# Front end of a fused attention and feed-forward kernel in another order: bv, AqT, Gram of batch 1, and x of batch 0 in two DMAs

## The chip, the core and the metric

The kernel runs on one NeuronCore of one Trainium2 chip; the seven others are idle. The metric is the device time of one execution in microseconds (us), lower is better. Times in the profile are in us from the start of the span, which is the time from the first to the last instruction.

## What is computed

The input x is [8, 1024, 128] (batch, sequence, channels), all in float32. A layer of linear attention and a feed-forward layer follow each other, each with a residual and a layer norm. Cut to what matters:

```python
q, k1, k2, v1, v2 = [heads(x + x @ W.T + b) for W, b in (...)]   # 16 heads of 8 channels
S1 = einsum('bhnd,bhne->bhde', k1, v1) / n                       # 8 x 8 for each head
S2 = einsum('bhnd,bhne->bhde', k2, v2) / n
S12 = S1 * S2
out = q @ S1 * mean(v2) * g1 + S12.sum(2) * g2 + q @ S2 * mean(v1) * g3 + q @ S12 * g4
a = layernorm(out) * ln_g + ln_b
x = layernorm(x + a @ Wo.T + bo)
tgt2 = relu(x @ w1[0] + b1[0]) @ w2[0] + b2[0]                   # the routing always picks expert 0
x = layernorm(x + layernorm(x + tgt2) * gamma + beta)
```

Neither k nor v is ever computed for a row of x. With A = I + W.T, S1 is made of A.T G A and the bias, where G = x.T x is the 128 x 128 Gram matrix of a batch, with the column sums of x beside it. So each batch has a small preparation (G, then E = G A plus a bias part, V the sums of v, S, a matrix M, and the folded matrix "PQ" for q and the output), and then a product of x with PQ for every row.

## The kernel before

**Tiling.** Each batch is 8 tiles of 128 rows; a step handles a group of 4 tiles (512 rows), 16 steps in all, from n = 0 to 15. They are preceded by two steps of preparation, n = -2 and n = -1, which are the front end. Every engine has its own instruction stream written by hand; what orders the streams among each other is semaphores alone. A float32 matmul or transpose on TensorE appears in the profile as two instructions, except the `transpose` calls, which are one instruction each.

**TensorE in step -2** (`body`, lines 1182 to 1203): ten warm-up matmuls on the identity (`keep_warm(10)`), as soon as `ident` is made; the Gram products of batch 0 for tiles 0 to 3 (`gram(0, ...)`, which waits for x of batch 0); the transposes of the four k and v weights (`turn_kv`); the Gram products of tiles 4 to 7; `gram_av(0)`, which multiplies G with A_kv; `turn_vectors` (waits for all small vectors: spreads the bv rows over 128 partitions by a product with ones, transposes the biases and spreads the g factors); `turn_x(0)`, four transposes of x for the first product; `turn_o` (Wo); `turn_late` (ln_g, ln_b, b1); `keep_warm(2)`; `ak_e(0)`, which gives the raw S; `output_rows`, two products from the turned Wo (u and zw); `gram(1)`, the Gram products of batch 1, in bank `up_ps[2]`; `attention_matrix(0)`, M with AqT; `gram_av(1)`; `centered(0)`, the product with the centering matrix, which gives PQ; `ak_e(1)`. In step -1 three tiles of `gram(2)` come before `product(0, 0)`, the first product of x with PQ, and then `turn_x(1)`, the rest of `gram(2)`, `gram(3)`, `attention_matrix(1)`, half of `gram(4)`, `centered(1)` and `turn_x1(0)`, which turns the normalized x1 for the feed-forward part.

**VectorE in step -2**: A_kv from the turned weights (lines 769 to 771); then it waits for `vec_turned` and copies g_rows and the first three columns of `cols`; `e_and_v(0)` (E, line 854, needs `bv_rows`, V, line 861, needs `nbv_rows`); `factors` (a column of AqT, line 779, the other columns of `cols`, and the sum AqT = Wq + I, line 783); `prepare(dve, 0)` (gv, then S of batch 0 in `s_out`, then S12, T, S12g and M); `u_row`, `xT_rest(0)`, `e_and_v(1)`, `PQ_rest(0)` (the two lower parts of PQ, lines 818 and 819), `s_out(1)`.

**ScalarE in step -2**: G of batch 0 to SBUF (`gram_out(0)`), the three copies of bv (`less_bv`), the upper part of x transposed (`xT_upper(0)`), `output_weights` (lnb_wide, WoT, Wog, and at its end the wait for zw and `center`), `gram_out(1)`, then the copy of PT (`PT_copy`) and of the upper part of PQ (`PQ_upper`).

**GpSimd**: constants, eight DMAs (Wo, Wq, bo, b2, beta, gamma, w1, w2), then the head mask times g (`gmask`, needs `cols_ready`), then x + u for the first two groups (`xu`), and the preparation of batch 1.

**DMA queues**: SyncE issues x of batch 0, Wk1, Wk2, ln_g, ln_b, b1 and x of batches 1 to 7, in this order. ScalarE issues Wv1, Wv2, bk1, bk2, bq, bv1, bv2 and four g vectors. The issuing instructions run in order on the engine's sequencer.

## Time and profile before

| what | value |
|---|---|
| median of 3 runs | 204.87 us (204.83 to 205.17) |
| profiled execution, its own time | 204.72 us |
| its span | 203.0 us |
| busy: TensorE matmul / VectorE / ScalarE / GpSimd | 94% / 78% / 64% / 70% |
| TensorE's share of the chain that ended last | 85% |
| memory traffic | 6.17 MB read, 4.20 MB written |

"Busy" is the share of the span in which an engine executes; waits are not in it. TensorE's matmul and its weight loads overlap each other, and matmuls are pipelined, so that the distance from one start to the next is shorter than one's duration. A row of the timeline merges like instructions that follow each other; the time in brackets is the idle time of the engine before the row, with the instruction that ended it. "SPq" and "ACTq" are the sequencers that issue DMAs.

### The profile page before, as it was taken

The numbers are of one execution on the slowest core, as the hardware profiler recorded it, in microseconds if no ns is written. First come the engines' busy times: TensorE is split into PE (matmuls) and PEld (weight loads), VectorE is DVE, ScalarE is ACT, GpSimd is POOL, SyncE is SP. The second block draws the span as 40 slices with busy tenths as digits, with TensorE's granted clock in tenths as the row PEclk, the third lists the DMA queues.
The fourth block names the chain that finished last, engine by engine and source line by source line (L and its number), as shares of the span: only waits on it lengthen the run. The fifth ranks groups of instructions, "written<-read, shape, count | busy, mean of one in ns | idle before, by whom it ended". The sixth has DMA issues, their size and how long they took to land.

```text
span 203.0 us, 4316 instructions
## 1 busy us (share of the span) xinstructions
PE 191.2 (94%) x1381; PEld 174.8 (86%) x1381; DVE 157.6 (78%) x471; ACT 129.2 (64%) x386; POOL 141.2 (70%) x190
## 2 busy tenths in 40 slices
PE   6899999999999999999999999999999999999920
PEld 6788997989898999999997989898989899987820
DVE  0186745987869887898879896989698969897683
ACT  0342538372859665975758675967597759786852
POOL 8526662676489838986599759985998598877350
PEclk9999999999999999999999999999999999999985
DMA  5999501200001000101001300100010101011012
GB/s 151 238 243 288 143 0 27 58 0 5 0 0 55 37 15 5 53 0 52 3 16 51 117 2 0 53 28 28 0 55 2 52 3 52 2 52 40 15 53 103
DMA packets 12624, 10.64 MB, mean 52 GB/s; under 512 B 713, under 2 KB 10458, under 8 KB 12602
## 3 DMA queue, kind: packets, MB, share of 16 engines
q1 hardware_dynamic: 11944, 9.32, 15.2%
q0 software_dynamic: 352, 0.92, 2.5%
q8 instruction: 11, 0.18, 0.4%
q10 hardware_dynamic: 306, 0.13, 0.2%
q14 instruction: 11, 0.09, 0.2%
HBM read 6.17 MB, written 4.20 MB: 51 GB/s over the span
## 4 chain that ended last, share of the span: by engine, by line
PE 85%; DVE 6%; issue 3%; ACT 2%; POOL 2%; DVEq 0%; POOLq 0%; ACTq 0%
PE up_ps L1024 26%; PE down_ps L1024 25%; PE z_ps L1024 14%; PE prep_ps L1024 12%; PE turn_ps L1177 4%; PE turn_ps L1148 3%; DVE st L793 1%; DVE down_ps L844 1%; POOL y2g L548 1%; POOL y L552 1%; DVE z_ps L904 1%; ACT res L667 1%; DVE y2n L800 1%; DVE res L1001 0%; DVE y L986 0%
## 5 line engine op out<-in xcount | busy, mean ns | idle before, releaser
L1024 PE MATMUL down_ps<-w_sb,hT 128*128 128x128 f32 x480 | 58.9, 276 | 0.1
L1024 PEld LDWEIGHTS down_ps<-w_sb,hT 128*128 128x128 f32 x480 | 56.4, 192 | 0.7 <-ACT hT L685 0.3
L685 ACT ACTIVATE hT<-up_ps,cols 128x512 f32<-128x512 f32 x64 | 42.2, 682 | 5.2 <-PE up_ps L1024 5.0
L667 ACT ACTIVATE res<-y,nb,rstd 128x128 f32<-128x128 f32 x60 | 24.8, 483 | 6.6 <-POOL nb L516 5.9
L574 POOL TENSOR_TENSOR x1b<-x,b_rows 128x512 f32<-128x512 f32 x16 | 20.5, 1284 | 10.6 <-DVE x L800 10.6
L1024 PE MATMUL up_ps<-x1T_hi,w_hi 128*128 128x512 f32 x64 | 26.1, 408 | 0.0
L1024 PE MATMUL up_ps<-x1T_lo,w_hi 128*128 128x512 f32 x64 | 25.4, 398 | 0.0
L1024 PE MATMUL up_ps<-x1T_hi,w_lo 128*128 128x512 f32 x64 | 25.3, 395 | 0.0
L548 POOL TENSOR_TENSOR y2g<-y2n,gamma_rows 128x512 f32<-128x512 f32 x15 | 19.2, 1281 | 4.9 <-DVE y2n L800 4.9
L800 DVE TENSOR_SCALAR x<-z_ps,st,rstd 128x128 f32<-128x128 f32 x64 | 21.9, 405 | 0.1
L634 ACT ACTIVATE z_sq<-z_ps 128x128 f32<-128x128 f32 x64 | 16.8, 270 | 7.6 <-PE z_ps L1024 7.6
L800 DVE TENSOR_SCALAR y2n<-down_ps,st,rstd 128x128 f32<-128x128 f32 x60 | 21.0, 405 | 0.5
L563 POOL TENSOR_TENSOR xu<-X,u_rows 128x512 f32<-128x512 f32 x16 | 18.9, 1186 | 3.2 <-DVE u_rows L789 3.2
L576 POOL TENSOR_TENSOR x1beta<-x,beta_rows 128x512 f32<-128x512 f32 x16 | 20.6, 1291 | 0.0
L552 POOL TENSOR_TENSOR y<-y2g,x1beta 128x512 f32<-128x512 f32 x15 | 19.1, 1272 | 1.2
L1024 PE MATMUL z_ps<-PQ_hi,xT_hi 128*128 128x256 f32 x64 | 19.3, 302 | 0.0
L904 DVE SCALAR_TENSOR_TENSOR z_ps<-z_ps,rstd,xu 128x128 f32<-128x128 f32 x64 | 18.2, 353 | 0.6
L1024 PE MATMUL z_ps<-PQ_hi,xT_lo 128*128 128x256 f32 x64 | 18.0, 282 | 0.0
L1024 PE MATMUL z_ps<-PQ_lo,xT_hi 128*128 128x256 f32 x64 | 17.9, 280 | 0.0
L1024 PE MATMUL z_ps<-PQ_hi,spread 128*128 128x256 f32 x64 | 17.9, 280 | 0.0
L626 ACT ACTIVATE std<-st,eps_col 128x4 f32<-128x4 f32 x46 | 12.4, 295 | 7.3 <-DVE st L793 7.3
L733 ACT ACTIVATE x1T_hi<-turn_ps 128x512 fp32r<-128x512 f32 x16 | 9.4, 589 | 11.1 <-PE turn_ps L1148 10.9
(170 smaller groups left out, 418.3 us busy)
## 6 DMA issues: line engine op xcount, KB each, us to landing
X<-in_L_attn_x SPq DMA_DIRECT2D x8, 512.0 KB, 8.7
out<-res SPq DMA_DIRECT2D x15, 256.0 KB, 2.0
V_all<-V_dram SPq DMA_DIRECT2D x6, 128.0 KB, 3.1
w_sb<-in_L_ffn_w POOLq DMA_DIRECT2D x2, 256.0 KB, 8.4
out<-res SPq DMA_DIRECT2D x2, 128.0 KB, 2.2
w_raw<-in_L_attn_Wv ACTq DMA_DIRECT2D x2, 64.0 KB, 2.7
w_raw<-in_L_attn_Wk SPq DMA_DIRECT2D x2, 64.0 KB, 3.9
w_raw<-in_L_attn_Wo POOLq DMA_DIRECT2D x1, 64.0 KB, 3.0
```

Source lines behind the costliest of these rows:

```text
L548: pool.tensor_tensor(y2g[:, :, :], y2n[:, :, :], rows(gamma_rows[:, :]), ALU.mult).then_inc(y2g_out, 1)
L552: pool.tensor_tensor(y3[(s - 1) % 2][:, :, :], y2g[:, :, :], x1beta[(s - 1) % 2][:, :, :], ALU.add).then_inc(y3_out, 1)
L563: pool.tensor_tensor(xu[s % 2][:, :, :], X[:, b, g * TILES:(g + 1) * TILES, 0:C], rows(u_rows[:, :]), ALU.add).then_inc(xu_out, 1)
L574: pool.tensor_tensor(x1b2[(s + 1) % 2][:, :, :], x1[:, :, :], rows(b2_rows[:, :]), ALU.add).then_inc(x1b2_out, 1)
L576: pool.tensor_tensor(x1beta[(s + 1) % 2][:, :, :], x1[:, :, :], rows(beta_rows[:, :]), ALU.add).then_inc(x1beta_out, 1)
L626: act.activation(dst[:, :], src, ACT.Sqrt, bias=eps_col[:, :], scale=scale).then_inc(done, 1)
L634: act.activation(z_sq[:, t, :], z_ps[t // 2][:, t % 2 * 256:t % 2 * 256 + C], ACT.Square, accum_out=z_sum[:, t:t + 1]).then_inc(sq_out, 1)
L667: last = act.activation(res[buf][:, t, :], y3[buf][:, t, :], ACT.Identity, scale=rstd4[:, t:t + 1], bias=nb4[:, t:t + 1])
L685: act.activation(hT[:, k, :], up_ps[k % len(up_ps)][:, :], ACT.Relu, bias=cols[:, 5 + k:6 + k]).then_inc(relu_out, 1)
L800: last = dve.tensor_scalar(dst[:, t, :], of_tile(t), st[:, t // 2, 3 * (t % 2) + 1:3 * (t % 2) + 2], rstd[:, t:t + 1], ALU.subtract, ALU.mult)
L904: last = dve.scalar_tensor_tensor(out=y1_tile(t), in0=y1_tile(t), scalar=rstd1[:, t:t + 1], in1=xu[(s + 1) % 2][:, t, :], op0=ALU.mult, op ...
L1024: return pe.matmul(o, lhsT, rhs, start=start, stop=stop)
```

## The change

- x of batch 0 is loaded by two DMAs of four tiles each. The second has its own semaphore, `x0_second`, which the second Gram half and GpSimd's second `xu` wait for.
- On ScalarE's queue the two bv rows are issued ahead of bk1, bk2 and bq, with their own semaphore; the product that spreads them (`spread_bv`) moves from `turn_vectors` to the place between the second Gram half and the wait for A_kv.
- TensorE: six warm-up matmuls instead of ten, `keep_warm(2)` gone, `turn_vectors` behind `turn_x(0)` and `turn_o`, `gram(1)` ahead of `output_rows`, `gram_av(1)` ahead of `attention_matrix(0)`, two tiles of `gram(2)` ahead of `centered(0)` and two behind `ak_e(1)` instead of three there.
- VectorE: g_rows and the first three columns of `cols` are copied after E and V of batch 0, S and S12 of batch 0 come before gv, and the column of AqT is copied between them.
- GpSimd computes the sum AqT = Wq + I, after its DMA issues and before `gmask`.
- ScalarE: `gram_out(1)` comes before the copy of zw to `center`.

```diff
+            def values():
+                eng.wait_ge(masks_ready, 1)
+                eng.tensor_tensor(gv[:, :, :], v_of(b), gmask[:, 0:2, :], ALU.mult).then_inc(m_step, 1)
+
+            def scores():
+                eng.wait_ge(S_out, b + 1)
+                eng.tensor_tensor(S12[:, :], S_sb[:, 0, :], S_sb[:, 1, :], ALU.mult).then_inc(m_step, 1)
+
             if b == 0:
                 s_out(eng, 0)
-            eng.wait_ge(S_out, b + 1)
-            eng.tensor_tensor(S12[:, :], S_sb[:, 0, :], S_sb[:, 1, :], ALU.mult).then_inc(m_step, 1)
+                scores()
+                eng.tensor_copy(AqT[:, C:C + 1], cols[:, 2:3]).then_inc(AqT_ready, 1)
+                values()
+            else:
+                values()
+                scores()
...
-            load_x(0)
+            half = SEQ_TILES // 2
+            sp.dma_start(X[:, 0, 0:half, 0:C], x_v[0, :, 0:half, :]).then_inc(x_loaded[0], 16)
+            sp.dma_start(X[:, 0, half:SEQ_TILES, 0:C], x_v[0, :, half:SEQ_TILES, :]).then_inc(x0_second, 16)
...
+            pool.wait_ge(consts, 2)
+            pool.wait_ge(qo_loaded, 16 * 2)
+            pool.tensor_tensor(AqT[:, 0:C], w_raw[:, 5, :], ident[:, :], ALU.add).then_inc(AqT_ready, 1)
             pool.wait_ge(const_set, 4)
...
+            for i, v in enumerate((bv1, bv2)):
+                act.dma_start(bv_row[:, i, :], row(v)).then_inc(bv_loaded, 16)
             for i, v in enumerate((bk1, bk2, bq)):
                 act.dma_start(vec_rows[i:i + 1, :], row(v)).then_inc(vec_loaded, 16)
-            for i, v in enumerate((bv1, bv2)):
-                act.dma_start(bv_row[:, i, :], row(v)).then_inc(vec_loaded, 16)
...
+            def center_weights():
+
                 act.wait_ge(zw_done, 1)
                 act.activation(center[:, 1, :], zw_ps, ACT.Copy).then_inc(zw_ready, 1)
...
                     gram_out(1)
+                    center_weights()
...
-            dve.wait_ge(vec_turned, 1)
-            dve.tensor_copy(g_rows[:, :, :].rearrange("p i h -> p (i h)"), vec_ps[:, 3:67])
-            dve.tensor_copy(cols[:, 0:3], vec_ps[:, 0:3]).then_inc(cols_ready, 1)
 
             def factors():
 
-                dve.wait_ge(cols_ready, 1)
-                dve.tensor_copy(AqT[:, C:C + 1], cols[:, 2:3])
+                dve.wait_ge(vec_turned, 1)
+                dve.tensor_copy(g_rows[:, :, :].rearrange("p i h -> p (i h)"), vec_ps[:, 3:67])
+                dve.tensor_copy(cols[:, 0:3], vec_ps[:, 0:3]).then_inc(cols_ready, 1)
                 dve.wait_ge(late_turned, 1)
                 dve.tensor_copy(cols[:, 3:9], late_ps).then_inc(late_ready, 1)
-                dve.wait_ge(qo_loaded, 16 * 2)
-                dve.tensor_tensor(AqT[:, 0:C], w_raw[:, 5, :], ident[:, :], ALU.add).then_inc(AqT_ready, 1)
+                dve.wait_ge(cols_ready, 1)
...
+            def spread_bv():
+
+                pe.wait_ge(bv_loaded, BV_VECTORS)
+                mm(bv_ps, ones[0:1, :], bv_row[:, :, :].rearrange("p j c -> p (j c)")).then_inc(bv_done, 1)
+
             def turn_vectors():
 
                 pe.wait_ge(vec_loaded, VECTORS)
-                mm(bv_ps, ones[0:1, :], bv_row[:, :, :].rearrange("p j c -> p (j c)")).then_inc(bv_done, 1)
...
-                    keep_warm(10)
+                    keep_warm(6)
                     pe.wait_ge(consts, 2)
                     gram(0, range(0, 4))
                     turn_kv()
                     gram(0, range(4, SEQ_TILES))
+                    spread_bv()
                     pe.wait_ge(A_ready, 1)
                     gram_av(0)
-                    turn_vectors()
                     turn_x(0)
                     turn_o()
+                    turn_vectors()
                     turn_late()
-                    keep_warm(2)
                     ak_e(0)
+                    gram(1, range(SEQ_TILES))
                     output_rows()
-                    gram(1, range(SEQ_TILES))
+                    gram_av(1)
                     attention_matrix(0)
-                    gram_av(1)
+                    pe.wait_ge(nbv_ready, 1)
+                    gram(2, range(0, 2))
                     centered(0)
                     ak_e(1)
                     return
                 if st.n == -1:
-                    pe.wait_ge(nbv_ready, 1)
-                    gram(2, range(0, 3))
+                    gram(2, range(2, 4))
                     product(0, 0)
                     turn_x(1)
-                    gram(2, range(3, SEQ_TILES))
+                    gram(2, range(4, SEQ_TILES))
```

## Rows read from the trace of the kernel before

**Rows 1.** Page: chain that ended last, shares by engine

```profile
PE 85%; DVE 6%; issue 3%; ACT 2%; POOL 2%; DVEq 0%; POOLq 0%; ACTq 0%
```

**Rows 2.** Timeline: start, us, engine, line, operation, tiles, count, [idle <-releaser]

```profile
0.94 0.64 SPq L430 DMA_DIRECT2D X<-in_L_attn_x  x1
...
1.58 4.28 PE L1024 MATMUL up_ps<-ident 128*128 128x128 f32 x20 [1.58 <-POOL ident L476]
...
1.63 1.11 SPq L436 DMA_DIRECT2D w_raw<-in_L_attn_Wk  x2
...
3.76 13.25 SPq L430 DMA_DIRECT2D X<-in_L_attn_x  x6
```

**Rows 3.** DMA issues: tile, queue, count, KB each, us from issue to landing

```profile
X<-in_L_attn_x SPq DMA_DIRECT2D x1, 512.0 KB, 4.9
...
w_raw<-in_L_attn_Wk SPq DMA_DIRECT2D x2, 64.0 KB, 3.9
...
X<-in_L_attn_x SPq DMA_DIRECT2D x1, 512.0 KB, 6.5
```

**Rows 4.** Timeline: Gram of batch 0, weight transposes, G out, gram_av(0)

```profile
5.95 1.13 PE L1024 MATMUL prep_ps<-X 128*128 128x130 f32 x8
...
6.92 0.60 PE L1034 MATMUL z_ps<-ident,w_raw 128*128 128x128 f32 x4
...
7.35 1.06 PE L1024 MATMUL prep_ps<-X 128*128 128x130 f32 x8
...
8.45 0.28 ACT L680 ACTIVATE G_sb<-prep_ps 128x130 f32<-128x130 f32 x1 [1.82 <-PE prep_ps L1024]
...
8.87 1.10 PE L1024 MATMUL prep_ps<-A_kv,G_sb 128*128 128x256 f32 x4 [0.46 <-ACT G_sb L680]
```

**Rows 5.** Timeline: bv products, E and V of batch 0

```profile
9.90 0.69 PE L1024 MATMUL up_ps<-bv_row,ones 1*128 1x256 f32 x2
...
11.13 0.48 DVE L854 SCALAR_TENSOR_TENSOR E_sb<-bv_rows,G_sb,prep_ps 128x256 f32<-128x256 f32 x1
...
11.53 0.42 DVE L861 TENSOR_TENSOR V_sb<-prep_ps,nbv_rows 128x256 f32<-128x256 f32 x1
```

**Rows 6.** Timeline: the last warm-up pair, AqT's column, ak_e(0)

```profile
11.66 0.71 PE L1024 MATMUL up_ps<-ident 128*128 128x128 f32 x4
...
11.86 0.14 DVE L779 COPY AqT<-cols 128x1 f32<-128x1 f32 x1
...
12.21 0.61 PE L1024 MATMUL prep_ps<-E_sb,A_kv 128*128 128x128 f32 x4
```

**Rows 7.** Timeline: mask on GpSimd; gv, S, T and M_sb on VectorE

```profile
11.37 1.07 POOL L505 TENSOR_TENSOR gmask<-g_rows,head_mask 128x512 f32<-128x512 f32 x1 [3.65 <-DVE cols L774]
...
12.55 0.43 DVE L372 TENSOR_TENSOR gv<-V_sb,gmask 128x256 f32<-128x256 f32 x1
...
12.93 0.61 DVE L359 SCALAR_TENSOR_TENSOR S_sb<-V_sb,cols,prep_ps 128x128 f32<-128x128 f32 x2
...
13.89 0.42 DVE L378 TENSOR_TENSOR T_sb<-S_sb,gv 128x256 f32<-128x256 f32 x1
...
15.01 0.29 DVE L383 TENSOR_TENSOR M_sb<-M_half,S12g 128x128 f32<-128x128 f32 x1
```

**Rows 8.** Timeline: attention matrix, PT, centered product, second PQ split

```profile
15.46 0.39 PE L1024 MATMUL prep_ps<-AqT,M_sb 128*128 128x130 f32 x2
...
16.00 0.28 ACT L654 ACTIVATE PT_sb<-prep_ps 128x130 f32<-128x130 f32 x1
...
16.95 1.03 PE L1024 MATMUL prep_ps<-center,PT_sb 128*128 128x256 f32 x4
...
19.10 0.43 DVE L819 TENSOR_TENSOR PQ_hi<-prep_ps,PQ_hi 64x256 fp32r<-64x256 f32 x1
```

**Rows 9.** Windows: stretch, us, busy by engine (instructions), PEclk, DMA share, GB/s

```profile
194.00:196.00 2.00, 0.19 (x2) 0.00 (x0) 1.60 (x5) 1.16 (x4) 0.98 (x3) 1.00 0.05 14
```

**Rows 10.** Timeline, TensorE's weight loads: transposes of x1 and their wait

```profile
26.91 0.42 PEld L1148 LDWEIGHTS turn_ps<-ident,x 128*128 128x128 f32 x4 [0.36 <-DVE x L800]
```

More of the change, by code:

```diff
@@ L175, in build @@
         kv_loaded = sem("kv_loaded")
+        bv_loaded = sem("bv_loaded")
         bv_done = sem("bv_done")
@@ L187, in build @@
         ffn_rows = sem("ffn_rows")
+        x0_second = sem("x0_second")
         x_loaded = [sem(f"x_loaded{b}") for b in range(BATCHES)]
@@ L369, in prepare @@
             wait(eng, pt_done, b)
-            eng.wait_ge(masks_ready, 1)
             k = b * 4
-            eng.tensor_tensor(gv[:, :, :], v_of(b), gmask[:, 0:2, :], ALU.mult).then_inc(m_step, 1)
+            def values():
[4 more added lines that the diff above has]
+                eng.tensor_tensor(S12[:, :], S_sb[:, 0, :], S_sb[:, 1, :], ALU.mult).then_inc(m_step, 1)
             if b == 0:
                 s_out(eng, 0)
-            eng.wait_ge(S_out, b + 1)
-            eng.tensor_tensor(S12[:, :], S_sb[:, 0, :], S_sb[:, 1, :], ALU.mult).then_inc(m_step, 1)
+                scores()
[4 more added lines that the diff above has]
+                scores()
             wait(eng, m_step, k + 2)
@@ L418, in run_steps @@
                 body(Step(n))
-        VECTORS = 16 * (4 + 3 + 2)
+        VECTORS = 16 * (4 + 3)
+        BV_VECTORS = 16 * 2
         LATE_VECTORS = 16 * 3
@@ L559, in body @@
                     pool.wait_ge(x_loaded[b], 16)
+                    if n == -1:
+                        pool.wait_ge(x0_second, 16)
                     if st.n == -2:
@@ L1063, in gram @@
                 pe.wait_ge(x_loaded[b], 16)
+                if b == 0 and tiles[0] >= SEQ_TILES // 2:
+                    pe.wait_ge(x0_second, 16)
                 if b == 3:
@@ L1120, in attention_matrix @@
                 wait(pe, M_out, (b + 1) * 2)
-                pe.wait_ge(AqT_ready, 1)
+                pe.wait_ge(AqT_ready, 2)
                 mm(prep_ps[:, 0:XW], M_sb[:, :], AqT[:, :], start=True, stop=False)
```

## The prediction

> **What bounds the kernel now.** I read the chain of work that ended last first: TensorE carries 85% of it [rows 1]. From about 28 us on TensorE has hardly a gap, so the steady state is a fixed amount of matmul work that starts when the front end lets it. The change touches the front end alone, and the amount of steady work is the same. So the question is by how much the first product on x (`product(0, 0)`) moves, and whether the shift survives until the dense part. Every time below is of the profiled execution, 204.72 us around its span of 203.0; the median of the runs shown is 204.87, 0.15 above it, and I subtract the shift from the median.
>
> Then I read the timeline of the front end by the row that each TensorE group waits for. In order: TensorE warms up on `ident` from 1.58 to 5.86, and x of batch 0 lands 4.9 after its issue at 0.94, at 5.84 [rows 2, 3]. The Gram products follow at 5.95, the four weight transposes at 6.92, the second half of the Gram at 7.35; G leaves ScalarE at 8.73 and lets `gram_av(0)` start at 8.87 [rows 4]. Behind it stand the bv products at 9.90; their copies hold back E until 11.13 and V until 11.53, 1.2 us after the products that E reads were over [rows 5]. Then comes a pair of warm-up matmuls, `ak_e(0)` at 12.21 [rows 6], VectorE's chain to M_sb at 15.30 [rows 7], and from M_sb the chain attention matrix, PT copy, centered product, PQ split, first product [rows 8]. Nearly all of it is one dependent chain of small steps, with TensorE, VectorE and ScalarE taking turns.
>
> **The change, part by part.**
>
> *x in two DMAs, ten warm-ups to six.* The first half must land before the transposes can be late because of it. The whole transfer takes 4.9 from issue, a transfer of 64 KB behind it 3.9 [rows 3]; so a half of 256 KB takes between 3.9 and 4.9, and lands at 4.8 to 5.8. The issue pitch of such a DMA is 0.69 (0.94 to 1.63) [rows 2], so Wk, the small rows and x of batches 1 to 7 are issued up to 0.69 later. Six warm-ups are twelve instructions at 4.28 / 20 = 0.214 each: TensorE is through at 4.2 and idle for 0.6 to 1.6. What binds next is `turn_kv`, which needs both Wk. Of the pair issued in 1.63 to 2.74 the second starts near 2.3 and lands 3.9 later, at 6.2 [rows 2, 3]. It stands behind x in the same queue, so either the queue's bytes set its landing (6.2 again) or its issue does (6.9). I take 6.2, since 64 KB taking 3.9 looks like waiting behind the 512 KB. The first Gram half is then hidden: from 4.8, eight instructions at 0.21 end at 6.5, at 0.11 at 5.7; with the clock rising in between as before, just under 6.2. The transposes start at 6.2 + 0.1 = 6.3 instead of 6.92, with the startup of the first one some 0.1 lost; the second Gram half comes at 6.82 instead of 7.35, and G and with it `gram_av(0)` at 8.35 instead of 8.87: **−0.52**. If Wk lands at 6.9, this step gives +0.1 to +0.2 instead. A_kv moves with the transposes and stays ahead of G, which is what the matmul row names as releaser [rows 4].
>
> The clock: the twenty warm-up instructions run at a pitch of 0.21, the later ones of the same kind at (7.35 − 6.92) / 4 = 0.11 [rows 2, 4], so TensorE starts at its 1.2 GHz level and gets to 2.4 GHz near the end of the warm-up. With six warm-ups it has a pause before that point. The trace of before has one telling stretch: at the end TensorE is busy for 0.19 of 2.00 us and its granted clock is still 1.00 [rows 9]; that is a pause that doesn't lower the clock, but not one that comes before it has risen. The Trainium skill ("TensorE: Matmul & The Clock Gate", What's actually happening) says that "the default state is throttled, and activity releases the throttle", which speaks against taking warm-ups away ahead of a pause. By that rule the time could be the one of the second rival below; the trace agrees that the start is at the low level, and shows nothing of a pause there. In the sum I take the rise at the same place as before, since the pause is short beside the 2.7 us of matmuls ahead of it and Gram work follows it.
>
> *bv in the wait for G.* The two bv products cost 0.69 with the tail, 0.5 of TensorE's order [rows 5]. They now stand between the last Gram instruction (about 7.7) and 8.35, where TensorE waits for G: 7.73 + 0.54 = 8.27, hidden by 0.1. Their DMAs are first of the small ones on ScalarE's queue; they are issued by 2.3 and, at Wk's 3.9 or even x's 4.9, land by 7.2; only x of batch 1's 6.5 [rows 3] would show. The bv copies on ScalarE lie under `gram_av(0)`. E then follows the products: 8.35 + 1.10 = 9.45, V 0.40 behind it and ready at 10.27 [rows 4, 5].
>
> *TensorE's order up to `ak_e(0)`.* Before, 3.34 from `gram_av(0)` to `ak_e(0)`. Gone are the bv products (0.5), the small idle time ahead of them (0.1) and `keep_warm(2)` (12.21 − 11.66 = 0.55) [rows 6]; `turn_vectors` behind `turn_x` and `turn_o` is only a new order. So 2.17, `ak_e(0)` at 10.5: **−1.70** in all. V with 0.15 of latency is there at 10.42, so the cover is thin: each delay of E or V beyond 0.1 shows.
>
> *Gram of batch 1 ahead of `output_rows`.* It wants x of batch 1 at 10.5 + 0.45 = 10.96. That landed at 3.76 + 6.5 = 10.26 [rows 2, 3], and with one more issue ahead of it between 10.26 and 10.95: no cost up to the last hundredth. Sixteen instructions take 1.79, the output rows 0.45 behind them, G of batch 1 is there 0.64 after the last Gram instruction, so `gram_av(1)` starts at 13.3 and TensorE is free at 14.25.
>
> *VectorE: S first, AqT's sum to GpSimd.* AqT's [128, 128] sum leaves VectorE before E or S is due, and GpSimd is idle there; its place ahead of the mask costs only if Wq, GpSimd's second DMA, landed after 10.4. S starts 0.7 after `ak_e(0)` (12.21 to 12.93) at 11.2 [rows 6, 7]. From S to T were 0.96; now the one-column copy (0.14 [rows 6]) and gv (0.4, formerly ahead of S) stand in between: 1.5, T at 12.75. From T to M_sb's end 1.41, so 14.15, and the attention matrix 0.15 later at 14.3, against 15.46: **−1.15**. This is the term that gives back 0.5 of the 1.70: the DVE order is not a gain in itself. The mask (1.07 on GpSimd) starts when cols are there, at 10.9, and ends at 12.0, before gv at 12.3 [rows 7].
>
> *From the attention matrix to the product.* Before, the centered product came 1.49 after the attention matrix, since `gram_av(1)` stood between, while PT was copied by 16.28. Now only PT's copy and two tiles of Gram of batch 2 (0.45, in that wait) do: 0.82 to the copy's end and 0.15, so 15.3 instead of 16.95: **−1.65**. V and S of batch 1 are behind u and xT_lo on VectorE as before and move with them. From the centered product to the end of the second PQ split are 2.58 [rows 8], a pure chain, with `ak_e(1)` and two tiles of Gram under it: the split ends at 17.9 against 19.53, and the product's fourth instruction, which needs it, follows at 18.0. The shift stays −1.65.
>
> *After it.* TensorE waited 0.36 for x1 [rows 10]; with one tile less behind the product it waits 0.22 more, but x1 itself moves with the product, so the dense part starts 1.65 earlier. Loads of x that land up to 0.7 later are used well after their landing.
>
> Sum: 204.87 − 1.65 = **203.2** (profiled execution 203.1).
>
> **Rivals.**
>
> 1. *The wait for Wk takes the place of x's.* Wk lands at 6.9, by its issue. Then the first step gives +0.15 instead of −0.52, the rest keeps its −1.1: 204.87 − 1.0 = **203.9**. For it: Wk is issued 0.69 later. Against: it stands behind x in the queue. Chance 0.12.
> 2. *The clock rises later*, only when the second Gram half is through, instead of near the end of the warm-up. Four transposes and eight Gram instructions ahead of G take 0.1 more each: +1.2, with rounding 204.87 − 0.4 = **204.5**. For it: a pause of 0.6 to 1.6 where there was none. Against: the late row with 1.00 over an idle stretch. Chance 0.10.
> 3. *Slower: the clock stays low until `ak_e(0)`.* The same mechanism further on: 1.2 up to G, 4 x 0.22 in `gram_av(0)`, and 13 instructions at 0.1 up to the end of `ak_e(0)` make 1.2 + 0.9 + 1.3 = 3.4, and the time is 204.87 − 1.65 + 3.4 = **206.6**. It decides from the point where more than 1.65 is lost, which is in the middle of `gram_av(0)`: a clock still at 1.2 GHz when E's products run. TensorE is busy by then, so chance 0.05.
> 4. *The gain isn't delivered*: something further on has its own limit, such as a load or the x1 chain, and TensorE waits there instead; 204.5 to **204.9**. Against: no TensorE wait after 20 us but the one for x1, which hangs on the product. Chance 0.08.
>
> The forecast has 0.65. **How the numbers follow.** Around it the small unknowns (x half 0.3, V's thin cover 0.2, x of batch 1 0.3, gv 0.2) make 202.8 to 203.7. The range must reach over the first rival and up to the second: 202.6 to 204.5. About 0.2% (0.41 us) is what a measurement can tell from no change, so faster is below 204.46: forecast, first rival, and part of the second: 0.82. The same: the rest of the second and the fourth: 0.12. Slower: 0.06.
>
> **What the profile after would show.** The kv transposes near 6.3 and nothing but kv ahead of them; the bv products before `gram_av(0)`, which starts near 8.35; E near 9.45; `ak_e(0)` near 10.5; M_sb's end near 14.15; the centered product near 15.3; the product's fourth instruction near 18.0 behind a wait for the PQ split; the x1 wait of TensorE near 0.6. A pitch of 0.21 in the transposes or the second Gram half would be the second rival; transposes at 7.0 the first. The prediction is wrong if the dense part doesn't start 1.2 to 2.0 earlier, or starts so and the end doesn't.

## The result, and the profile after

| | before | after |
|---|---|---|
| median | 204.85 us (204.74 to 205.17, 4 runs) | 202.90 us (202.24 to 203.10, 4 runs) |
| ratio to before | | 0.9891, 95% interval 0.9872 to 0.9911 |
| profiled execution | 204.72 us, span 203.0 | 202.93 us, span 201.2 |

The kernel is faster by about 2.2 us by the ratio, 1.95 by the medians, 1.8 in the profiled spans. The forecast was 203.2, 1.65 faster. A second set of six runs of the same kernel gave 202.66 us and 0.9887 (0.9866 to 0.9908).

The page of the kernel after: span, TensorE's row (busy us, share, instructions), and the chain that ended last.

```profile
span 201.2 us, 4296 instructions
...
PE 190.6 (95%) x1369; PEld 174.4 (87%) x1369; DVE 156.9 (78%) x470; ACT 129.1 (64%) x386; POOL 141.6 (70%) x191
...
PE 86%; DVE 6%; issue 3%; POOL 2%; ACT 1%; DVEq 0%; POOLq 0%
```

TensorE has 12 instructions less (six pairs of warm-up) and 0.6 us less busy time, but the span is 1.8 shorter. So most of the gain is time in which TensorE waited. Now the timeline of the start, which answers [rows 2, 4, 5]: start, duration, engine, line, operation, count.

```profile
0.94 0.44 SPq L449 DMA_DIRECT2D X<-in_L_attn_x  x1
...
1.44 0.49 SPq L450 DMA_DIRECT2D X<-in_L_attn_x  x1
...
1.58 2.93 PE L1045 MATMUL up_ps<-ident 128*128 128x128 f32 x12 [1.58 <-POOL ident L492]
...
1.98 0.99 SPq L452 DMA_DIRECT2D w_raw<-in_L_attn_Wk  x2
...
4.30 1.94 PE L1045 MATMUL prep_ps<-X 128*128 128x130 f32 x8
...
6.04 1.10 PE L1055 MATMUL z_ps<-ident,w_raw 128*128 128x128 f32 x4
...
6.93 1.17 PE L1045 MATMUL prep_ps<-X 128*128 128x130 f32 x8
...
8.03 0.69 PE L1045 MATMUL up_ps<-bv_row,ones 1*128 1x256 f32 x2
8.13 0.28 ACT L703 ACTIVATE G_sb<-prep_ps 128x130 f32<-128x130 f32 x1 [1.76 <-PE prep_ps L1045]
...
8.65 1.13 PE L1045 MATMUL prep_ps<-A_kv,G_sb 128*128 128x256 f32 x4
```

Three things are to be seen. The first Gram half starts at 4.30 right behind the warm-up, with no pause. It and the transposes run at the slow pitch: (6.04 − 4.30) / 8 = 0.22, and (6.93 − 6.04) / 4 = 0.22, where the transposes of before had 0.11 [rows 4]. The record of the granted clock in this trace begins at 7.1; in the trace of before it does at 5.35. (The windows view prints a PEclk of 1.00 ahead of that record as well, so at the start the record and the pitch count, and not PEclk.) And the bv products are nearly hidden: G is out at 8.41 and `gram_av(0)` starts at 8.65. Before, it started 0.14 behind G (8.73 and 8.87) [rows 4]; now it follows the bv products, 0.1 later than that.

The DMA view by issues (KB each, us from issue to landing) answers [rows 3]: the first half of x, Wk, x of batch 1.

```profile
X<-in_L_attn_x SPq DMA_DIRECT2D x1, 256.0 KB, 2.9
...
w_raw<-in_L_attn_Wk SPq DMA_DIRECT2D x2, 64.0 KB, 3.2
...
X<-in_L_attn_x SPq DMA_DIRECT2D x1, 512.0 KB, 6.1
```

The half is there 2.9 after its issue, at 3.84. Each half occupies SyncE for 0.50 (0.94 to 1.44), not the 0.69 of the whole, so Wk is issued only 0.35 later and x of batch 1 0.20 later.

The rest of the chain, which answers [rows 5 to 8], and the first x1T_lo, behind which the dense part begins:

```profile
9.82 0.48 DVE L875 SCALAR_TENSOR_TENSOR E_sb<-bv_rows,G_sb,prep_ps 128x256 f32<-128x256 f32 x1 [1.69 <-PE prep_ps L1045]
...
10.22 0.42 DVE L882 TENSOR_TENSOR V_sb<-prep_ps,nbv_rows 128x256 f32<-128x256 f32 x1
...
10.78 0.68 PE L1045 MATMUL prep_ps<-E_sb,A_kv 128*128 128x128 f32 x4
...
11.60 0.61 DVE L361 SCALAR_TENSOR_TENSOR S_sb<-V_sb,cols,prep_ps 128x128 f32<-128x128 f32 x2 [0.45 <-PE prep_ps L1045]
...
12.96 0.42 DVE L391 TENSOR_TENSOR T_sb<-S_sb,gv 128x256 f32<-128x256 f32 x1
...
14.08 0.29 DVE L396 TENSOR_TENSOR M_sb<-M_half,S12g 128x128 f32<-128x128 f32 x1
...
14.59 0.39 PE L1045 MATMUL prep_ps<-AqT,M_sb 128*128 128x130 f32 x2
...
15.13 0.28 ACT L677 ACTIVATE PT_sb<-prep_ps 128x130 f32<-128x130 f32 x1 [1.11 <-PE prep_ps L1045]
...
15.55 0.67 PE L1045 MATMUL prep_ps<-center,PT_sb 128*128 128x256 f32 x2
...
17.78 0.43 DVE L840 TENSOR_TENSOR PQ_hi<-prep_ps,PQ_hi 64x256 fp32r<-64x256 f32 x1
...
26.69 0.69 DVE L963 TENSOR_TENSOR x1T_lo<-turn_ps,x1T_hi 128x512 fp32r<-128x512 f32 x1 [1.38 <-ACT x1T_hi L757]
```

All further readings use one anchor: the start of `gram_av(0)`. Up to it, DMA landings and the clock decide; behind it the steps are so regular that their distance from the anchor is the same within 0.03 from one trace to another, unless something was changed or a load of x came late (which happened in "after, again" and "no warm-up"). The times in the table are read from the timelines of all kernels of this study, `ak_e(0)` and the later columns as distance from the anchor; "clock" is where the trace's record of the granted clock begins, as a time of the span.

| kernel | clock | gram_av(0) | ak_e(0) | S starts | M_sb ends | centered | PQ split ends | first x1T_lo | median us |
|---|---|---|---|---|---|---|---|---|---|
| before | 5.35 | 8.87 | 3.34 | 4.06 | 6.43 | 8.08 | 10.66 | 19.37 | 204.85 |
| before, again | 5.47 | 8.83 | 3.33 | 4.05 | 6.42 | 8.08 | 10.65 | 19.36 | |
| after | 7.14 | 8.65 | 2.13 | 2.95 | 5.72 | 6.90 | 9.56 | 18.04 | 202.90 |
| after, again | 5.17 | 7.93 | 2.13 | 2.95 | 5.72 | 7.22 | 9.80 | 18.27 | 202.66 |
| one DMA | 10.53 | 11.42 | 2.13 | 2.95 | 5.72 | 6.90 | 9.56 | 18.04 | 205.07 |
| one DMA, ten warm-ups | 6.44 | 9.38 | 2.13 | 2.95 | 5.72 | 6.91 | 9.56 | 18.04 | 203.83 |
| two DMAs, ten warm-ups | 7.38 | 9.62 | 2.14 | 2.95 | 5.73 | 6.91 | 9.56 | 18.06 | 203.78 |
| no warm-up | 7.82 | 8.93 | 2.13 | 2.95 | 5.73 | 7.43 | 10.08 | 18.58 | 203.86 |
| bv behind | 7.34 | 8.64 | 3.21 | 4.03 | 6.80 | 7.99 | 10.64 | 19.13 | 203.62 |
| gv first | 5.34 | 8.15 | 2.13 | 4.03 | 6.40 | 7.52 | 10.17 | 18.65 | 203.13 |
| TensorE's old order | 5.84 | 8.07 | 2.14 | 2.96 | 5.73 | 7.38 | 9.96 | 18.64 | 202.96 |
| warm-up pair | 4.52 | 8.39 | 2.60 | 3.34 | 6.11 | 7.45 | 10.11 | 18.58 | 203.17 |
| further | 6.74 | 8.44 | 1.70 | 2.52 | 5.33 | 6.80 | 9.38 | 18.06 | 202.38 |
| further, tiles behind | 7.74 | 8.92 | 1.70 | 2.52 | 5.33 | 6.80 | 9.38 | 18.29 | 203.14 |

From x1T_lo on, both kernels run in step: the first one comes at 28.24 and 26.69, the last at 186.91 and 185.40, so the shift is 1.55 at the start of the dense part and 1.51 at its end. Another 0.29 arises behind that, in the tail (below). In the two profiled executions the 1.8 are thus 0.22 up to the anchor, 1.10 from the anchor to the PQ split, 0.23 from there to x1T_lo, and 0.25 net behind it: 0.29 in the tail, less 0.04 on the way.

### The profile page after: what moved, and what is told of

The parts are those of the page before. It is cut to its first block, busy times and chain, and to the rows that moved or that the text cites. A ratio compares the mean times of both kernels' runs of the same rounds, so it can differ in the third digit from the quotient of the medians.

```text
span 201.2 us, 4296 instructions
## 1 busy us (share of the span) xinstructions
PE 190.6 (95%) x1369; PEld 174.4 (87%) x1369; DVE 156.9 (78%) x470; ACT 129.1 (64%) x386; POOL 141.6 (70%) x191
## 2 busy tenths in 40 slices
DMA packets 12641, 10.64 MB, mean 53 GB/s; under 512 B 730, under 2 KB 10475, under 8 KB 12619
## 4 chain that ended last, share of the span: by engine, by line
PE 86%; DVE 6%; issue 3%; POOL 2%; ACT 1%; DVEq 0%; POOLq 0%
PE down_ps L1045 25%; PE up_ps L1045 25%; PE z_ps L1045 14%; PE prep_ps L1045 13%; PE turn_ps L1204 3%; PE turn_ps L1175 3%; DVE st L814 1%; DVE down_ps L865 1%; POOL y2g L567 1%; POOL y L571 1%; DVE z_ps L925 1%; ACT res L690 1%; DVE y2n L821 1%; PE z_ps L1055 0%; DVE res L1022 0%
```

## Experiments

Each kernel is the kernel after with the edit shown; ratios are to the kernel before. Not undone by themselves were the order of ScalarE's DMA queue, the sum for AqT on GpSimd, the later place of `turn_vectors`, and ScalarE's `gram_out(1)` ahead of the copy of zw.

### x of batch 0 in one DMA

```diff
-            half = SEQ_TILES // 2
-            sp.dma_start(X[:, 0, 0:half, 0:C], x_v[0, :, 0:half, :]).then_inc(x_loaded[0], 16)
-            sp.dma_start(X[:, 0, half:SEQ_TILES, 0:C], x_v[0, :, half:SEQ_TILES, :]).then_inc(x0_second, 16)
+            load_x(0)
```

(and both waits for `x0_second` gone)

> The kernel after with x of batch 0 loaded by one DMA again; nothing else changed. In the trace of the kernel after, the first half of the Gram products started at 4.30 right behind the warm-up and ran at a pitch of 0.215, and the clock rose only at 7.1. Theory (the split buys time on the way to G): TensorE pauses from 4.3 to about 5.9 and the weight transposes come at 6.9 to 7.7 instead of 6.04, G and gram_av(0) 0.3 to 1.3 later than 8.65, and the time is 203.2 to 204.2 against 202.9. Rival (the first half only fills a wait that Wk sets, and the clock sets the rest): gram_av(0) within 0.1 of 8.65 and 202.9. On the clock: if a pause of 1.6 keeps it low, the pitch is 0.21 up to 8.0 or later, and the time is above 204.2.

Measured: 205.07 us over 10 runs (203.52 to 205.70), ratio 1.0004 (0.9982 to 1.0026): with this one part undone the whole gain is gone. The start in its timeline:

```profile
1.58 2.93 PE L1041 MATMUL up_ps<-ident 128*128 128x128 f32 x12 [1.58 <-POOL ident L490]
...
6.41 2.07 PE L1041 MATMUL prep_ps<-X 128*128 128x130 f32 x8 [1.90 <-DMA X<-in_L_attn_x]
...
8.27 1.06 PE L1051 MATMUL z_ps<-ident,w_raw 128*128 128x128 f32 x4
...
9.12 1.74 PE L1041 MATMUL prep_ps<-X 128*128 128x130 f32 x8
...
11.42 1.13 PE L1041 MATMUL prep_ps<-A_kv,G_sb 128*128 128x256 f32 x4
```

TensorE stands from 4.5 to 6.41, and then the Gram half has a pitch of (8.27 − 6.41) / 8 = 0.23, the transposes 0.21, the second half (9.12 to the bv products at 10.80, eight) 0.21. The granted clock rises at 10.5. Behind the anchor nothing differs from the kernel after by more than 0.01. So all of it lies ahead of the anchor, and there the profiled execution has 11.42 against 8.65. That the time goes above 204.2 was expected for the case that a pause keeps the clock low; both the theory's range and the rival's were too small. Single times reach from 203.52 to 205.70, a wider spread than in any other kernel here (1.8 without warm-up, at most 1.2 in the rest). That fits a late rise that isn't there in each execution, but only one execution of it has a trace.

### One DMA, ten warm-ups, and two DMAs, ten warm-ups

```diff
-                    keep_warm(6)
+                    keep_warm(10)
```

The first on the one-DMA kernel, the second on the kernel after.

> The kernel after with one DMA for x of batch 0 and ten warm-up matmuls: the one-DMA kernel with its pause ahead of x filled again. That kernel with six warm-ups had a clock that rose at 10.5 and a median of 205.07. Theory (the pause between warm-up and x kept the clock low, and that is what cost 2.1): without the pause the clock rises by 7.4, the transposes come near 6.9, gram_av(0) near 8.9, and the time is 203.6, as with two DMAs and ten warm-ups. Rival (the single DMA itself costs it, by a later x and a later Wk): 204.6 to 205.1.

> The kernel after with ten warm-up matmuls instead of six, x still in two DMAs. Theory (the first Gram half now has a slot of its own before Wk lands, and more warm-up pushes it out of that): at a clock that rises near 5.3 the warm-up ends at 5.86, the Gram half at 6.85, the transposes run then instead of at 6.05 and gram_av(0) starts at 8.85 as in the kernel before (8.87), where the runs with an early rise had 8.07 to 8.15: 0.7 later, 203.6 against 202.9. Rival (longer warm-up makes the clock rise sooner or more surely and gives that back): 202.9 or less.

Measured: 203.83 us (203.54 to 204.09), 0.9943 (0.9924 to 0.9961) for one DMA; 203.78 us (203.51 to 204.08), 0.9941 (0.9922 to 0.9960) for two. Both theories hold in direction and time (203.6 expected for each). The anchors are 0.5 and 0.8 later than they said (9.38 and 9.62, for 8.9 and 8.85), since the clock rose at 6.44 and 7.38 and not near 5.3. The one-DMA kernel with the pause filled:

```profile
1.58 4.64 PE L1041 MATMUL up_ps<-ident 128*128 128x128 f32 x20 [1.58 <-POOL ident L490]
...
6.29 1.21 PE L1041 MATMUL prep_ps<-X 128*128 128x130 f32 x8
...
7.33 0.60 PE L1051 MATMUL z_ps<-ident,w_raw 128*128 128x128 f32 x4
...
9.38 1.13 PE L1041 MATMUL prep_ps<-A_kv,G_sb 128*128 128x256 f32 x4
```

Against the kernel with six warm-ups the anchor is 2.04 earlier and the median 1.24 lower, though four pairs of matmuls were added that compute nothing. x landed hardly sooner in it (5.2 after its issue against 5.3). The clock rose 4.1 earlier in it (6.44 and 10.53). So what the pause cost in the one-DMA kernel was the clock. And with ten warm-ups it makes no difference whether x comes in one DMA or two (203.83 and 203.78). The two edits are worth nothing or less each by itself: six warm-ups alone 205.07, two DMAs alone 203.78, neither 203.83, both together 202.90 and 202.66. The rival of the second one, that more warm-up makes the clock rise more surely early, falls: it rose at 6.44 and 7.38.

### No warm-up

```diff
-                    keep_warm(6)
+                    keep_warm(0)
```

> The kernel after without any warm-up ahead of the first Gram half. TensorE then starts at 4.0, when the first half of x is there, and hardly pauses from then on. Theory (TensorE's work from 1.58 on is what brings the clock up in time): the first Gram half still ends before Wk lands, so nothing is later by the work itself, but the clock rises later than 7.3; every instruction up to the rise costs 0.1 to 0.2 more, gram_av(0) starts at 9.4 or later instead of 8.1 to 8.65, and the time is 204 to 206. Rival (the clock rises by itself at the place it did, whatever TensorE does before): 202.9.

Measured: 203.86 us (203.77 to 205.61), ratio 0.9964 (0.9926 to 1.0003). Two rows of its timeline, the first Gram half and Gram of batch 1:

```profile
4.13 2.07 PE L1045 MATMUL prep_ps<-X 128*128 128x130 f32 x8 [4.13 <-DMA X<-in_L_attn_x]
...
12.00 2.06 PE L1045 MATMUL up_ps<-X 128*128 128x130 f32 x16 [0.26 <-DMA X<-in_L_attn_x]
```

The clock rose at 7.8 in the profiled execution, hardly later than with warm-up, and the anchor is at 8.93, not at 9.4 or later: this part of the theory missed. A kernel with warm-up and its rise at 7.74 (the last of the table) has the anchor at 8.92, the same. One of four times is 205.61, which a still later rise would make, but no trace shows that. 0.5 of the profiled execution's loss is something else: behind the anchor x1T_lo comes at 18.58 instead of 18.04, since Gram of batch 1 waits for its x (the row says so), which here took 8.0 from issue to landing, against 6.1 in the kernel after. What the warm-up itself is worth stays open between these two.

### bv behind gram_av(0)

```diff
-                    spread_bv()
                     pe.wait_ge(A_ready, 1)
                     gram_av(0)
+                    spread_bv()
```

> The kernel after with the two bv products behind gram_av(0) instead of in the wait for G. Theory (they delay E and V through the bv copies): bv products at 9.3, their copy on ScalarE at 10.0 to 10.1, E at 10.5 instead of 9.82, V ready at 11.3, ak_e(0) at 11.45 instead of 10.78, everything behind it 0.6 to 0.7 later: 203.5 to 203.6. Rival (only TensorE's own order counts, and the wait for G is simply moved): TensorE has 0.5 less ahead of G and 0.5 more behind it, and V's wait takes it up: no more than 0.2 later, 203.1.

Measured: 203.62 us (203.09 to 204.03), 0.9929 (0.9903 to 0.9956). The chain from bv to `ak_e(0)` in its timeline:

```profile
9.67 0.69 PE L1045 MATMUL up_ps<-bv_row,ones 1*128 1x256 f32 x2
...
10.40 0.38 ACT L630 ACTIVATE bv_rows<-up_ps 128x256 f32<-128x256 f32 x1 [1.91 <-PE up_ps L1045]
...
10.89 0.48 DVE L875 SCALAR_TENSOR_TENSOR E_sb<-bv_rows,G_sb,prep_ps 128x256 f32<-128x256 f32 x1 [2.80 <-ACT bv_rows L630]
...
11.85 0.68 PE L1045 MATMUL prep_ps<-E_sb,A_kv 128*128 128x128 f32 x4 [0.35 <-DVE V_sb L882]
```

The bv products, ScalarE's copy, E and V follow each other, and E is at 10.89 instead of 9.82, so TensorE now waits for V (the 0.35 in brackets). All columns behind the anchor are 1.08 to 1.09 later up to x1T_lo; the theory had the mechanism and 0.65 for its size. It expected E at 10.5 from products at 9.3. They started at 9.67: `gram_av(0)` holds TensorE for 1.03 ahead of them (8.64 to 9.67, as 8.87 to 9.90 before [rows 4, 5]). The copy followed their end (9.67 + 0.69 = 10.36) as expected. The medians show 0.7 to 1.0 of the 1.09, and the intervals overlap at their ends, so the size rests on the trace.

### gv ahead of S

```diff
-                s_out(eng, 0)
-                scores()
                 eng.tensor_copy(AqT[:, C:C + 1], cols[:, 2:3]).then_inc(AqT_ready, 1)
                 values()
+                s_out(eng, 0)
+                scores()
```

> The kernel after with gv of batch 0 ahead of S and S12 on VectorE, and the one-column copy ahead of both. Theory (the order on VectorE was part of the gain once the mask became late): gv waits for GpSimd's mask, ready at 12.29, so gv is done at 12.85 and S starts near 12.75 instead of 11.60; from S to T 0.96: T at 13.7 instead of 12.96, the attention matrix 0.7 later, 203.6. Rival (S first costs what it brings, as the sum of the prediction had it, which put 1.5 between S and T): T within 0.2 of 12.96, 203.0.

Measured: 203.13 us (202.84 to 203.73), 0.9912 (0.9886 to 0.9939). gv and S in its timeline:

```profile
11.84 0.42 DVE L376 TENSOR_TENSOR gv<-V_sb,gmask 128x256 f32<-128x256 f32 x1 [1.07 <-POOL gmask L524]
12.18 0.60 DVE L361 SCALAR_TENSOR_TENSOR S_sb<-V_sb,cols,prep_ps 128x128 f32<-128x128 f32 x2
```

gv waits for the mask, S stands behind it and starts 4.03 after the anchor instead of 2.95; x1T_lo is 0.61 later. The medians show 0.2 to 0.5 of it. So once E and V are early the order on VectorE is part of the gain, since the mask from GpSimd is the later of the two inputs. By time alone it can't be told from nothing.

### TensorE's old order behind ak_e(0)

```diff
-                    gram(1, range(SEQ_TILES))
                     output_rows()
-                    gram_av(1)
+                    gram(1, range(SEQ_TILES))
                     attention_matrix(0)
-                    pe.wait_ge(nbv_ready, 1)
-                    gram(2, range(0, 2))
+                    gram_av(1)
                     centered(0)
...
-                    gram(2, range(2, 4))
+                    pe.wait_ge(nbv_ready, 1)
+                    gram(2, range(0, 4))
                     product(0, 0)
```

> The kernel after with TensorE's order behind ak_e(0) as in the kernel before: output rows, Gram of batch 1, attention matrix, gram_av(1), centered, with the four tiles of Gram of batch 2 all behind ak_e(1). Theory (this order is worth what it takes out from between the attention matrix and the centered product): Gram of batch 1 is through at 13.6, the attention matrix waits for M_sb and starts at 14.55, gram_av(1) follows in the wait for PT at 14.95, the centered product starts at 15.9 instead of 15.55: 0.3 to 0.4 later, 203.2 to 203.3. Rival (the chain on VectorE and ScalarE sets the product in either order): 202.9. Second rival (the reordering is the larger part of the gain): 203.9.

Measured: 202.96 us (202.82 to 203.63), 0.9905 (0.9883 to 0.9927). By the trace the centered product is 0.48 later behind the anchor, the PQ split 0.40, x1T_lo 0.60. The median is within 0.3 of the kernel after, and the intervals overlap, so by time alone this part can't be told from nothing; the anchored distance says it is worth 0.4 to 0.6 when no load is late, as the theory had it. The second rival, with 203.9, falls.

### A warm-up pair put back

```diff
                     turn_late()
+                    keep_warm(2)
                     ak_e(0)
```

> The kernel after with keep_warm(2), four instructions on TensorE, put back ahead of ak_e(0). Theory (TensorE has nothing to wait for there): ak_e(0) starts 2.6 after gram_av(0) instead of 2.13, and the first x1T_lo comes 18.5 after gram_av(0) instead of 18.04: 0.45 slower, 203.2 against 202.8. Rival (V, which is ready 1.95 after gram_av(0), or the mask sets the pace): 0.1 slower at most.

Measured: 203.17 us (202.92 to 203.54), 0.9910 (0.9889 to 0.9930). `ak_e(0)` 2.60 behind the anchor, x1T_lo 18.58: 0.54 later, as the four instructions take. TensorE has nothing to wait for there. Its median is 0.3 to 0.5 above the kernel after, with overlapping intervals. The same trace has the earliest rise of the clock, at 4.52, and yet its anchor is at 8.39, later than with a rise at 5.17 (7.93) in the table:

```profile
6.28 0.66 PE L1055 MATMUL z_ps<-ident,w_raw 128*128 128x128 f32 x4 [0.81 <-DMA w_raw<-in_L_attn_Wk]
```

With an early clock the first Gram half is over before Wk lands, and Wk sets the transposes. In the kernel after with its rise at 7.1 they stand behind the Gram half, and no wait is named.

### The kernel after once more, and the kernel before once more

No edit.

> The kernel after once more, unchanged, as a second sample and as the thing to compare the next ones with. The clock rose at 7.1 in its first profiled execution and between 5.3 and 7.4 in those of the kernels that share its first 8 us. Theory (the rise falls at a random place of that stretch from one execution to the next, and the work ahead of it sets the spread): gram_av(0) starts between 8.05 and 8.75, always 18.0 to 18.1 ahead of the first x1T_lo, single times 202.2 to 203.2, median 202.6 to 202.9. Rival (the rise belongs to the kernel): gram_av(0) at 8.65 again.

> The kernel before once more, unchanged, for a second look at its clock. In the first profiled execution the clock rose at 5.35 and gram_av(0) started at 8.87. Theory (the rise is random there too): if it comes at 5.9 or earlier gram_av(0) starts at 8.87 again, if it comes at 7.4 near 9.6, and in either case the first x1T_lo is 19.37 behind it and the time is between 204.6 and 205.5. Rival (ten warm-ups make the rise early each time): 8.87 again.

Measured: 202.66 us (202.26 to 203.37, 6 runs) for the kernel after; 204.75 us in one execution of the kernel before. The start of the kernel after, with the clock rising at 5.17:

```profile
4.31 1.48 PE L1045 MATMUL prep_ps<-X 128*128 128x130 f32 x8
...
5.82 0.66 PE L1055 MATMUL z_ps<-ident,w_raw 128*128 128x128 f32 x4
...
6.32 1.06 PE L1045 MATMUL prep_ps<-X 128*128 128x130 f32 x8
...
7.93 1.13 PE L1045 MATMUL prep_ps<-A_kv,G_sb 128*128 128x256 f32 x4
...
14.62 0.68 PE L1045 MATMUL up_ps<-X 128*128 128x130 f32 x4 [0.25 <-DMA X<-in_L_attn_x]
```

The same first half takes 1.51 instead of 1.74, the transposes 0.50 instead of 0.89, and the anchor is at 7.93 instead of 8.65: the place of the rise is not a property of the kernel, and the rival (8.65 again) falls. The theory was a little too narrow, too: it had the anchor between 8.05 and 8.75. Over the traces with warm-up and without a pause it lay between 4.5 and 7.7. For the kernel before both samples have it near 5.4 and the anchor at 8.87 and 8.83; its single times reach from 204.45 to 205.47, so a later rise there is possible but not shown, and the one trace decides between neither theory nor rival.

The last row is news: with the anchor this early, Gram of batch 2 (its two tiles ahead of the centered product) waits 0.25 for its x. The centered product comes 7.22 behind the anchor instead of 6.90, x1T_lo 18.27 instead of 18.04. A third of the clock's 0.72 is taken back by a load.

### Further, and further with two tiles behind the product

```diff
-                    turn_x(0)
-                    turn_o()
                     turn_vectors()
                     turn_late()
                     ak_e(0)
+                    turn_x(0)
+                    turn_o()
                     gram(1, range(SEQ_TILES))
                     output_rows()
-                    gram_av(1)
                     attention_matrix(0)
-                    pe.wait_ge(nbv_ready, 1)
-                    gram(2, range(0, 2))
+                    gram_av(1)
                     centered(0)
...
-                    gram(2, range(2, 4))
+                    pe.wait_ge(nbv_ready, 1)
+                    gram(2, range(0, 4))
                     product(0, 0)
...
-            return up_ps[1] if b == 1 else prep_ps
+            return up_ps[1] if b < 2 else prep_ps
```

(`ak_e(0)` doesn't wait for V, and the column of AqT is copied ahead of S. The second kernel has `gram(2, range(0, 2))` ahead of the product and the other six tiles behind it.)

> A version that goes further: turn_vectors and turn_late right behind gram_av(0), then ak_e(0) in a bank of its own so that it need not wait for V, turn_x and turn_o behind it, the attention matrix ahead of gram_av(1) again, the column of AqT copied ahead of S. Theory (the chain S, M, PT, PQ sets the product, and TensorE only has to keep out of its way): S starts 2.4 after gram_av(0) instead of 2.95, M_sb is done 5.2 after it instead of 5.7, the first x1T_lo comes 17.5 after gram_av(0) instead of 18.04, and the time is 202.4. Rival (TensorE's own work between gram_av(0) and the product is the bound by now): 18.0 and 202.9.

> The version that went further, with two of the four tiles of Gram of batch 2 moved from ahead of the first product to behind it. In that version the first x1T_lo came 18.06 after gram_av(0), as in the kernel after, though M_sb was 0.4 earlier. Theory (TensorE's own work between gram_av(0) and the product was its bound): with 0.45 less of it the product starts as soon as PQ is split, x1T_lo comes 17.85 to 17.95 after gram_av(0), and the wait of TensorE for x1 takes back less than that: 0.1 to 0.2 faster than the kernel after. Rival (no more than the chain of VectorE and ScalarE is left): 18.05 again and no difference.

Measured: 202.38 us (202.08 to 202.77, 4 runs), 0.9873 (0.9854 to 0.9893), and 203.14 us (202.34 to 203.49, 6 runs), 0.9898 (0.9878 to 0.9919). Two rows of the first, `ak_e(0)` and the weight loads of `ak_e(1)`:

```profile
10.14 0.71 PE L1045 MATMUL up_ps<-E_sb,A_kv 128*128 128x128 f32 x4
...
16.38 0.52 PEld L1045 LDWEIGHTS up_ps<-E_sb,A_kv 128*128 128x128 f32 x4 [0.51 <-DVE E_sb L875]
```

The median came out as the theory said, but not by the theory: S and M_sb are 0.4 earlier behind the anchor and x1T_lo is not (18.06), so the theory's 17.5 missed and its rival's 18.0 is what the trace shows. `ak_e(0)` went from 2.13 to 1.70, then `ak_e(1)` waited for E and V of batch 1 (the 0.51 in brackets), and four tiles of Gram stood between it and the product. Its anchor at 8.44 against 8.65 is the clock's work. Its lead over the kernel after in the median, 0.3 to 0.5, is no more than the spread of one kernel, and the intervals overlap, so no version of this study is shown to beat the kernel after.

The second missed: 18.29 instead of 17.9. The PQ split ended 9.38 behind the anchor in both, and the product's fourth instruction, which needs it, came at 9.43 instead of 9.74. But the 0.45 moved behind it delayed x1T_lo by 0.23 against the first; the reason stands under "Behind the product" below.

## Why the prediction was right, and where its steps were off

The time, 202.9, lies in the range of 202.6 to 204.5, and the direction and the place of the gain were right. That the sum came so near is partly luck. In the profiled execution the PQ split, where the forecast ends, is 1.32 earlier (19.53 and 18.21), not the 1.63 of the forecast; 0.23 behind the product and 0.25 behind that were not in the sum, and together they make the 1.80. Step by step:

**x in two DMAs, six warm-ups.** Forecast −0.52 at the anchor, measured −0.22 with a clock that rose at 7.1 and −0.94 (8.87 to 7.93) with one that rose at 5.2. The mis-sized term is the landing of the half: it was bounded by 3.9 and 4.9 from issue and took 2.9. The 3.9 was the time of a 64 KB transfer standing behind the 512 KB one in the same queue; it was a wait, and no lower bound for a transfer at the head of the queue. From this came a pause of 0.6 to 1.6 that doesn't exist in the kernel after. Wk was taken at 6.2 and the transposes behind it at 6.3. They started at 6.04 with the late clock, where the Gram half ahead of them sets them, and at 5.82, 6.05 and 6.28 in the three traces with the earliest rises (5.17, 5.34, 4.52), where Wk does. The anchor is at 7.93, 8.15 and 8.39 in these, against 8.35 forecast: at a like clock the step is worth between the forecast and 0.4 more, by the landing of Wk. The late rise takes 0.72 of the 0.94 back. The rival's 6.9 was wrong in both its terms: the halves are issued every 0.50, and Wk took 3.2 from issue, not 3.9.

**The clock, second and third rival.** The mechanism is real, but not in this kernel: there is no pause here. In the one-DMA kernel there is one, of 1.9, and the clock rose at 10.5; its median is 205.07, where the second rival had 204.5 and the third 206.6 for their cases. At the low level (1.2 GHz) TensorE's pitch in these rows is 0.21 to 0.23, at the high one (2.4 GHz) 0.11 to 0.12. The Trainium skill ("TensorE: Matmul & The Clock Gate", What's actually happening) with "activity releases the throttle" agrees with these traces: filling the pause with four more warm-ups brought the rise from 10.5 to 6.4. What the prediction left out is that the rise moves from execution to execution by over 2 us even without a pause, and that the trace of before, with a rise at 5.35, was one draw. "In the sum I take the rise at the same place as before" is the step that failed: the profiled execution has 0.3 less than forecast at the anchor, the one with the early rise 0.4 more.

**bv in the wait for G.** Forecast as hidden with 0.1 to spare; it lacks 0.1. `gram_av(0)` starts 0.62 behind the bv products (8.03 and 8.65, 7.31 and 7.93), not behind G, and 1.61 behind a second Gram half at full clock (6.32 and 7.93), where the kernel before has 1.52. The bv rows landed in time in every trace. Undone, it costs 1.09.

**TensorE's order up to `ak_e(0)`.** Forecast 2.17 behind the anchor, measured 2.13. V is the input that comes last by a hair, as said. Of this the pair of warm-ups is 0.5 and bv 1.1, measured one by one; they overlap.

**VectorE.** From S to T 1.5 forecast, 12.96 − 11.60 = 1.36 measured; S to the end of M_sb 2.77 against 2.95 forecast. S started 2.95 behind the anchor, forecast 2.85. "The order is not a gain in itself" was too low: undone alone it costs 0.6, since with an early V the mask is the later input.

**From the attention matrix to the product.** Centered product: forecast 6.95 behind the anchor (15.3 − 8.35), measured 6.90. PQ split: 9.55 forecast, 9.56 measured. This is the part that carries the gain, 1.10 of it. That it came out to the hundredth is luck in the last step: the centered product is 0.05 ahead of the forecast, and from there to the split it took 2.66 (15.55 to 18.21) and not 2.58. Nor was M_sb the last input, as the forecast had it: M_sb ends 5.72 behind the anchor, and the attention matrix starts at 5.94, when TensorE is through with `gram_av(1)`. In the kernel after, TensorE's own work sets the stretch from `ak_e(0)` to the centered product, which is why the warm-up pair costs its full 0.5.

**Behind the product.** The forecast held that x1 sets the place, that one tile less there only lengthens TensorE's wait of 0.36, and that this wait would be near 0.6. Its row has 0.37 in the kernel after, and x1T_lo moved 0.23 more than the PQ split. Two things were wrong. First, the 0.36 of [rows 10] is the idle time of the weight loads, not of the matmuls: the last of the four centered matmuls starts at 25.93 + 3 x 0.22 = 26.59 and holds TensorE until 26.8, and the transposes start at 26.91. The hole was 0.1, before and after. Second, x1 itself hangs on TensorE's work, through the order on ScalarE. The copy of G of batch 3 and the standard deviation for x1 behind it, before and after:

```profile
24.78 0.28 ACT L680 ACTIVATE G_sb<-up_ps 128x130 f32<-128x130 f32 x1 [1.51 <-PE up_ps L1024]
...
24.96 0.29 ACT L626 ACTIVATE std<-st,eps_col 128x4 f32<-128x4 f32 x1
```

```profile
23.23 0.28 ACT L703 ACTIVATE G_sb<-up_ps 128x130 f32<-128x130 f32 x1 [1.51 <-PE up_ps L1045]
...
23.40 0.29 ACT L649 ACTIVATE std<-st,eps_col 128x4 f32<-128x4 f32 x1
```

ScalarE waits 1.51 for the Gram products of batch 3, and the standard deviation stands behind that copy, though its statistics are ready at 24.56 in the kernel before. From this copy to x1T_lo are 3.45 to 3.48 in all fourteen traces. So a tile of Gram moved from behind the product to ahead of it brings x1 forward by its 0.22. The kernel with two tiles moved behind the product shows the same from the other side. The standard deviation ahead of the copy was not tried.

**The tail.** Not forecast at all: 0.29, of which 0.24 is in one wait. The statistics on y3 of the last but one group, VectorE, in the kernel before and in the kernel after:

```profile
194.35 0.76 DVE L793 BATCH_NORM_STATS2 st<-y 128x6 f32<-128x256 f32 x2 [0.27 <-POOL y L552]
```

```profile
192.59 0.76 DVE L814 BATCH_NORM_STATS2 st<-y 128x6 f32<-128x256 f32 x2
```

Both wait for GpSimd's y, which ends at 194.07 and at 192.55. The kernel before starts 0.28 behind that, the kernel after 0.04. The span behind the last x1T_lo is 16.07 in both traces of before and 15.78 to 15.83 in all twelve of the others, with the same instructions in it. What causes it stays open; no experiment went for it.

**Rivals.** Wk taking the place of x: it does bind the transposes when the clock rises early, but at 5.8 to 6.3, not at 6.9. A load further on: x of batch 2 took 0.25 in one execution, of 202.47 us. Both inside the range.

## What to carry to other kernels

Warm-up and first data are one edit: fewer warm-ups pay only when the data come early enough that TensorE doesn't stand between them, and a pause of 1.9 in that place cost 1.2 us here, about as much as the rest of the reordering brings (204.85 to 203.83). When a change moves the start of a long regular part, measure each of its parts as a distance from one common event; the distances repeat to 0.03, unless a load comes late, where the total spreads by 0.9. An engine that takes its work in order ties streams together that share no data: look at what stands ahead of the small step that the next stage waits for. A hole in a dense engine must be read from the matmul rows, not from the weight loads, and the latency of a transfer from one that stood at the head of its queue.

## What the runs showed of the hardware

- The granted clock of TensorE rose 2.9 to 6.2 us after the first matmul (4.5 to 7.7 on the timeline, first matmul at 1.58) in the twelve traces with warm-up and without a pause, with no relation to six or ten warm-ups, at 10.5 in the one with a pause of 1.9 behind the warm-up, and at 7.8 without warm-up, 3.7 after the first matmul. Single times of one changed kernel with warm-up and without a pause spread by 0.6 to 1.2 us, and the anchor by 0.72 between two traces of the same kernel.
- From SyncE, 256 KB at the head of the queue landed 2.9 to 3.1 after issue, 512 KB 4.8 to 5.3, and occupied the issuing engine for 0.44 and 0.64. The same 512 KB of batch 1, further back in the queue, took 6.0 to 8.1.
- A wait of 0.27 to 0.28 for a semaphore, in the tail, which one program shows in each trace and another with the same instructions there never does.
